# Copying the keys of one image by twelve two-dimensional transfers on one queue, instead of eight and four three-dimensional ones on two

## The reference

```python
h = tokens(x)                                  # 196 patches of 768 values -> 192, a class token, positions
h = h + attention(layernorm(h))                # 12 heads of 16, each query sees 13 neighbouring keys
h = h + experts(layernorm(h))                  # 8 experts 192 -> 768 -> 192, the best 2 per token

scores = einsum('bnhd,bnwhd->bnhw', q, k_win) * scale      # k_win: keys n-6 .. n+6
p      = softmax(where(valid, scores, -max))
out    = einsum('bnhw,bnwhd->bnhd', p, v_win) @ w_proj + b_proj
```

## Time and profile before

| what | value |
|---|---|
| median of 3 runs | 1888.35 us (1887.83 to 1889.15) |
| the profiled execution's own time | 1887.49 us |
| its span, first to last instruction | 1885.7 us |
| mean granted TensorE clock | 0.936 |
| exponentials (one per image), first and last start | 57.7 and 1064.1 us |
| busy: PE, PEld, DVE, POOL, ACT | 87%, 72%, 66%, 59%, 41% |

### The profile page before, as it was taken

One profiled execution on the slowest core, in us unless ns is written; L12 is line 12 of the kernel. 1 busy time (PEld: TensorE's weight loads), 2 busy tenths in 40 slices (PEclk: granted clock), 3 DMA queues, 4 the chain that ended last, 5 costly groups with the idle time before them and its releaser, 6 DMA issues. The chain is left out here.

```text
span 1885.7 us, 57924 instructions
## 1 busy us (share of the span) xinstructions
PE 1635.0 (87%) x19910; PEld 1361.4 (72%) x19911; DVE 1237.3 (66%) x3136; ACT 772.1 (41%) x1339; POOL 1104.6 (59%) x1020
## 2 busy tenths in 40 slices
PE   5668989888989798889898509999999999999995
PEld 4567878777868687778786406777777777777774
DVE  3567677677767677677676635666666666666663
ACT  2444444444434344344344305444444444444441
POOL 3226777767767677677677653455555555555554
PEclk8879999999999999999998759999999999999998
DMA  5453444444444444444444233443443444444332
GB/s 184 149 169 94 110 108 118 110 95 111 116 95 116 106 100 110 104 109 119 95 113 126 69 88 91 63 58 61 61 63 57 62 62 58 61 61 63 56 48 30
DMA packets 223375, 172.99 MB, mean 92 GB/s; under 512 B 142590, under 2 KB 197088, under 8 KB 222176
## 3 DMA queue, kind: packets, MB, share of 16 engines
q1 hardware_dynamic: 120752, 100.80, 20.5%
q0 software_dynamic: 74544, 42.61, 16.8%
q10 hardware_dynamic: 27904, 27.14, 4.8%
HBM read 94.76 MB, written 65.08 MB: 85 GB/s over the span
## 5 line engine op out<-in xcount | busy, mean ns | idle before, releaser
L376 POOL DMA_INDIRECT sorted_scratch<-payload,place x256 | 414.6, 1620 | 68.0 <-issue 67.3
L970 POOL DMA_INDIRECT out<-y,token x219 | 369.0, 1685 | 73.8 <-issue 73.2
L1078 PE MATMUL down<-w_hi,g_hi 128*128 x1314 | 323.6, 246 | 1.9 <-DVE y L1044 1.1
L1080 PE MATMUL down<-w_hi,g_lo 128*128 x1314 | 323.0, 246 | 0.0
L1079 PE MATMUL down<-w_lo,g_hi 128*128 x1314 | 322.9, 246 | 0.0
L756 PE MATMUL near<-we,patches 128*100 128x192 f32 x1536 | 279.2, 341 | 33.0 <-issue 24.6
L756 PEld LDWEIGHTS near<-we,patches 128*100 128x100 f32 x1536 | 256.6, 174 | 48.6 <-issue 45.9
L1066 PE MATMUL up<-e_xT,w_hi 128*128 128x384 f16 x1314 | 286.0, 327 | 0.2 <-ACT act_out L991 0.2
L991 ACT ACTIVATE act_out<-up,bias 128x384 f32<-128x384 f32 x438 | 251.2, 582 | 72.3 <-PE up L1066 72.2
L983 ACT COPY e_xT<-turned 128x1152 f16<-128x1152 f16 x73 | 81.7, 1119 | 362.6 <-PE turned L1058 362.6
L1027 DVE TENSOR_TENSOR g_lo<-act_out,g_hi 128x768 f16<-128x768 f32 x219 | 209.9, 959 | 7.6
(11 more groups left out here) (154 smaller groups left out, 3218.1 us busy)
## 6 DMA issues: line engine op xcount, KB each, us to landing
patches<-in_xt SPq DMA_DIRECT2D x64, 600.0 KB
rows<-sorted_scratch SPq DMA_DIRECT2D x73, 301.5 KB, 2.8
v_diag<-v_scratch SPq DMA_DIRECT2D x192, 78.1 KB
v_scratch<-v_rows SPq DMA_DIRECT2D x64, 159.4 KB
stage<-in_w ACTq DMA_DIRECT2D x8, 1152.0 KB
k_diag<-qk SPq DMA_DIRECT2D x512, 12.5 KB
out<-h ACTq DMA_DIRECT2D x64, 75.0 KB
out<-h ACTq DMA_DIRECT2D x64, 72.8 KB
```

The costliest lines, as they stand in the source:

```text
L376: pool.indirect_dma_start(out=sorted_dram, out_offset=bass.IndirectOffsetOnAxis(ap=at, axis=0), in_=payload[0:rows, 2 * image + n, :], in_ ...
L970: pool.indirect_dma_start(out=out, out_offset=bass.IndirectOffsetOnAxis(ap=token[k][:, n:n + 1], axis=0), in_=y[k % 2][:, n, :], in_offset ...
L1078: pe.matmul(dst, g_hi[k % 2][:, m, cols], high, start=(m == 0), stop=False)
L1080: ins = pe.matmul(dst, g_lo[k % 2][:, m, cols], high, start=False, stop=(m == MF - 1))
```

## The change

Both `qk16` and `k_diag` are laid out anew: the high and the low half of one chunk (or head) now stand behind one another in each partition, so that a head's keys, high and low, are one contiguous run of 222 + 200 = 422 values. The 22 values between the halves are zeros in `qk16` (from its memset at the start) and fall on the border columns of `k_diag`, which are to be zero. `qk16` has rows of 222 instead of 212 values. All twelve transfers of an image are issued by SP; ACT's loop of four, with its wait, is gone. ACT's and DVE's copies and PE's matmuls index the new order.

```diff
-        qk16 = [sb(f"qk16_{k}", [128, 2, 3, QUERY_WIDTH], F16) for k in range(2)]
-        k_diag = sb("k_diag", [128, 2, HEADS, KEY_WIDTH], F16)
+        qk16 = [sb(f"qk16_{k}", [128, 3, 2, KEY_WIDTH], F16) for k in range(2)]
+        k_diag = sb("k_diag", [128, HEADS, 2, KEY_WIDTH], F16)
...
-                    for h in range(8):
-                        to = DH * h
-                        sp.dma_start(k_diag[to:to + DH, :, h, REACH:REACH + SPAN],
-                                     qk16[(k - 3) % 2][to:to + DH, :, 1, 0:SPAN]).then_inc(s["k_diag_set"], 16)
+                    both = KEY_WIDTH + SPAN
+                    for h in range(HEADS):
+                        chunk, at = (1, DH * h) if h < 8 else (2, 64 + DH * (h - 8))
+                        to = DH * (h % 8)
+                        halves = qk16[(k - 3) % 2][at:at + DH, chunk].rearrange("p w n -> p (w n)")
+                        sp.dma_start(k_diag[to:to + DH, h].rearrange("p w n -> p (w n)")[:, REACH:REACH + both],
+                                     halves[:, 0:both]).then_inc(s["k_diag_set"], 16)
...
-                if runs(t, 2):
-
-                    if runs(t, 3):
-                        act.wait_ge(s["max_set"], 2 * a)
-                    else:
-                        act.wait_ge(s["qk_lo_set"], a + 1)
-                    for h in range(8, HEADS):
-                        to = DH * (h - 8)
-                        act.dma_start(k_diag[to:to + DH, :, h, REACH:REACH + SPAN],
-                                      qk16[k % 2][64 + to:64 + to + DH, :, 2, 0:SPAN]).then_inc(s["k_diag_set"], 16)
...
-                    act.copy(qk16[(k - 1) % 2][:, 0, :, 0:SPAN], qk[:, 0:3, 0:SPAN]).then_inc(s["qk_hi_set"], 1)
+                    act.copy(qk16[(k - 1) % 2][:, :, 0, 0:SPAN], qk[:, 0:3, 0:SPAN]).then_inc(s["qk_hi_set"], 1)
...
-                    dve.tensor_tensor(qk16[(k - 1) % 2][:, 1, :, 0:SPAN], qk[:, 0:3, 0:SPAN], qk16[(k - 1) % 2][:, 0, :, 0:SPAN],
+                    dve.tensor_tensor(qk16[(k - 1) % 2][:, :, 1, 0:SPAN], qk[:, 0:3, 0:SPAN], qk16[(k - 1) % 2][:, :, 0, 0:SPAN],
...
-                                        ins = pe.matmul(dst.rearrange("p (h c) -> p h c", c=KEYS), qk16[k % 2][:, of_q, chunk, at:at + 32],
-                                                        k_diag[:, of_k, heads, at:at + KEYS], start=False, stop=closes)
+                                        ins = pe.matmul(dst.rearrange("p (h c) -> p h c", c=KEYS), qk16[k % 2][:, chunk, of_q, at:at + 32],
+                                                        k_diag[:, heads, of_k, at:at + KEYS], start=False, stop=closes)
```

## The result

The changed kernel takes **1937.24 us** (four runs, 1936.65 to 1947.95), the kernel before 1888.74 in runs beside it: ratio 1.0271, 95% interval 1.0235 to 1.0307. It is 2.7% slower, where 1834 us was forecast, and outside the range. The profiled execution's span is 1935.1 us.

A forecast was written before the change was run, and what follows sets the result against it. In odd steps ACT's sequencer, issuing key transfers, was taken to hold back the exponential and PE; even steps gain nothing. 21 odd steps x 2.6 us = 54.6 us off 1887.49 gave 1834 us, range 1804 to 1878.

The forecast's parts named there:

- ACT's exponential: In odd steps it starts when DVE's subtraction ends, no longer held by ACT's four key issues: 1.7 us earlier.
- the links behind POOL's subtraction: In odd steps everything that follows POOL's subtraction, the payload's turning on PE first, comes 1.2 us earlier.
- the clock at its upper level: With no PE wait above 1 us, the work behind takes 2.1 us rather than 3.6: another 1.4 us per odd step.
- Layout and strides: New strides of copies and PE's reads: no change taken, 0.1 us a step either way, 6 us, for the range.
- the end of the chain: DVE waits 2.40 us for the logits in odd steps, so the whole 2.6 us reaches the next step.
- SP issues twelve transfers instead of eight: The price of the change, on SP's queue: 0.6 us more issuing per step, within two deadlines, so cost taken as nothing.
- The price of an issue: Each two-dimensional key issue on SP priced at the median patch load, 0.434 us; twelve take 5.7 us.
- the transfers are not cheaper: Rival, chance 0.13: issues stay at 0.594 us, keys or patches come late, odd steps lose 1.2 us; 1859 us.
- The landing: Keys land 2.8 us after issue, as for a larger load: at K + 8.5, K being when the maxima are done.
- The deadlines: Odd step: keys before the scores at K + 9.7, patches before the embedding at K + 11.2; margins 1.2 and 1.4 us.
- The rival on the slow side: Rival, chance 0.08: loaded queues raise an issue above 0.75 us, keys late in every step; 1906 us at 0.78.
- The rule I weighed: By the skill's rule, moving four issues from ACT to SP is worth about nothing; the 2.83 us trace row outweighed it.

The follow-up runs named there:

- scatters of 100 rows and the patches first: Changed kernel, with second-tile scatters of 100 rows instead of 97 and SP loading the next image's patches ahead of the keys: 1790.46 us, ratio 0.9491 to the kernel before.
- ten and two: Changed kernel with ten key transfers on SP, two on ACT, and the patches' load ahead of the keys: 1839.72 us with 97-row scatters, 1764.79 with 100.
- eight and four: Changed kernel with eight key transfers on SP, four on ACT, and the patches' load ahead of the keys, scatters of 97 rows: 1877.20 us.
- twelve: Changed kernel, all twelve key transfers on SP, with the patches' load issued ahead of the keys, scatters of 97 rows: 1928.75 us, ratio 1.0232 to the kernel before.

## Why the prediction was wrong

**What held.** ACT's exponential 1.7 us earlier; the links behind POOL's subtraction 1.4 us earlier, where 1.2 was forecast; the clock at its upper level behind it and 2.01 us for the work that took 3.62. PE's wait for the exponential fell under 25 us. Layout and strides cost nothing; they gained 0.4%, 9 us, a little more than the 6 us I allowed. And the end of the chain is borne out in part: with scatters of 100 rows and the patches first, 45 of the 54.6 us reach the time, though PE still waits 28.6 us for keys.

**The step that failed** is "SP issues twelve transfers instead of eight", whose cost was taken as nothing. Its three terms, in the step shown:

- *The price of an issue.* I took 0.434 us, the patches' median, "as the nearest two-dimensional transfer", so 5.7 us for twelve. The median is 0.589 us, and twelve take 7.9 us here, 8.1 in the median of the steps between 100 and 1000 us: above even my upper bound of 7.6. The rival "the transfers are not cheaper" had the issue's price right, at 0.13. The row of the same transfer in its old form was nearer than one of another kind.
- *The landing.* I added a constant 2.8 us, from one row of a 301 KB load. In the kernel before the last key landed 2.0 us behind SP's last issue in the median, so the constant was no bad guess there. In the changed kernel there are two kinds of step, 1.2 and 4.8 us in the median, parted by the end of POOL's first long scatter. This is the largest part: with 1.2 us the keys of the step shown would be in at K + 9.1, 0.2 us after PE is ready for them, and not at K + 12.7. That is also why the rival's 1859 us was wrong, for all that its price was right: it had the keys in at K + 10.4.
- *The deadlines.* PE is ready for the keys at K + 8.9, and not at K + 9.7. Some 0.5 us of that is a misreading: PE's wait for the keys stands ahead of the bias matmuls (L865, at 602.01 us in the kernel before), and I took the start of the score matmuls behind them (L876, 602.55). The rest is that the chain was shortened by 3.0 us to the value product, and not by 2.6. The patches, forecast to land in time, cost 31.6 us of waiting.

The rival on the slow side had the right mechanism, keys late, and the right sign at 0.08, but the wrong reason: it asked for issues of 0.75 us and a loss in every step. The issues' median didn't rise, and twelve of them take 0.68 us each with what lies between (8.1 us in all). What rose was the time behind them, in every second step, by the long scatter's rows, which travel one after another. That scatter stood in the trace of before (two kinds of L376, of 1.0 and 2.2 us), and the prediction doesn't name it.

**The rule I weighed.** The Trainium skill says in "DMA: Bandwidth & Descriptors", section "Issuing engines are not separate DMA queues", that a second issuing engine saves only the sequencer's time, usually small. Here that time is 0.59 us an issue, and giving two of twelve back to ACT is worth 26 us with 100 rows and 89 us with 97, where it also takes 20 steps back over the edge. So the row was rightly set above "usually", but I used it for the engine that lost four issues and not for the one that got them.

**Left open.** Why the rows of 97 travel one after another where those of 96 and 100 go side by side, and what the small packets are for. POOL's own longer work is not what delays the keys, since in the 32 steps whose last issue came before its end they landed in 1.2 us. But 96 and 100 rows shorten that work too, by some 1.1 us a scatter, and how much of the gain in time comes from it, in the kernel before above all, was not taken apart. With 100 rows PE still waits 32.4 us for the keys of twelve issues. They land 1.2 to 3.2 us behind the last issue in the 33 steps whose scatter ended first, 1.8 in the median. By the same estimate as above the length of the issues is 9.7 of the 32.4 us, and the rest is landings later than 1.2 us; what holds those was not tested. Nor is it known why an issue with eight partitions costs more than one with sixteen.

## What to carry to other kernels

Price an issue by the same transfer as it is now, not by a prettier one, and check where the last of them lands against a chain that you have just shortened: the wait that you remove can come back at whatever stood next. Look at how long an indirect scatter takes and how many packets it makes, and try a neighbouring number of rows, even where their engine is not the bound; one row of 97 cost the kernel before about what the change was forecast to gain. And split issues between queues by trying the numbers between all and none: ten and two was better than eight and four and than twelve by 2% and 5% with scatters of 97 rows.

## What the hardware showed that I had not expected

- An indirect scatter of 97 rows takes 2.2 us of GpSimd and 256 packets more than one of 96, which takes 1.0 us; one of 100 takes 1.0 us. In the kernel before that alone is worth 2.7%.
- Issuing a copy inside SBUF costs SP 0.59 us with two dimensions or three, and 0.625 us with half the partitions and bytes (medians).
- The rows of such a scatter of 97 travel one packet after another, 4.3 us from the first to the sixteenth; with 96 rows the sixteen start within 0.16 us.
- In the changed kernel a key transfer lands 1.2 us behind its issue (median of 32 steps) as long as POOL is not through with its scatter of 97 rows, and 4.8 us behind it (26 steps) once it is. What holds it comes after the scatter's instruction and not during it.
